# Local attention layers: the probabilities are turned in 32x32 blocks by VectorE and by DMAs through DRAM, with a new step order on every engine

## The chip, the core and the metric

The kernel runs on one core of one Trainium2 chip. The metric is the device time of one execution in microseconds (us). TensorE is PE, VectorE DVE, ScalarE ACT, GpSimd POOL, and SyncE (SP) issues the DMAs.

## The reference, cut to what matters

```python
x = x + 0.5 * ffn(layernorm(x))          # "ffn": two local layers
x = x + attn(layernorm(x), weight)       # global attention, 16 heads of 16
x = x + 0.5 * ffn(layernorm(x))
# one local layer, x of 8 x 512 x 256, 8 heads of 64, blocks of 128 tokens:
q, k, v = split(shift_token(x) @ wqkv)
q, k = rotary_xpos(l2norm(q) * qs, l2norm(k) * ksc)
sim  = q * 8 @ k.T      # a block of queries sees its own block of keys and the one before
attn = softmax(where(mask, -max, sim))
x    = x + (attn @ v) @ wo
h    = layernorm(shift_token(x)) * lg + lb
a, g = split(h @ w1 + b1);  x = x + (a * gelu(g)) @ w2 + b2
```

Everything is float32. Matrix products of weights are made of three products of rounded halves (`three`: hi by hi, lo by hi, hi by lo), the products inside attention of one float32 product.

## The kernel before

The kernel has three stages: a call of the two local layers, the global attention, and the local layers again. A local call is 16 rounds; a round is one sequence of 512 tokens through one layer, so rounds 0 to 7 are layer 1 and 8 to 15 layer 2. Rounds 3 to 6 and 9 to 14 are loops, the others are written out.

Within a round every engine works through a table of steps (`PE_STEPS`, `ACT_STEPS`, `DVE_STEPS`, `POOL_STEPS`). A name is a kind of step and a number; `+` marks a step of the next round, `-` one of the round before. So the attention of round n, the projections of round n+1 and the feed-forward part of round n-1 lie in one another. An engine keeps to its table strictly, and semaphores tie the tables together. The steps that matter here:

- z: PE turns x (bank for `zh`, `zl`, which split it into halves on ACT and DVE). q, k, v: projections, six products of 512 columns each. Q, K: PE turns the rotated q and k; `Qc`, `Kc` copy them out on ACT.
- sq, sk, ss: squares (ACT) and their sums (DVE). p: `rinv`, a power, on POOL. rq, rk: rotary on DVE. b, d: the sum of its two parts on POOL. c: k times `rinv`, on DVE (L1089).
- Attention goes by eight units i, each two heads by two query blocks; an even unit has 3, an odd one 4 blocks of 128x128 per head. S: scores on PE (L1514). X: mask and row maximum on DVE (L1106). E: exp on ACT (L848). R: reciprocal on DVE. N: scaling of the probabilities on POOL (L703). T: PE turns the 6 or 8 blocks into two PSUM banks (L1524). H, L: ACT (L855) and DVE (L1125) copy one bank each into `pT`. A: attn @ v on PE (L1544). O, P: its halves; W: times wo.
- n: PE turns the normalised rows; nh, nl: halves; x, l, r, j: residual and layer norm on DVE, s: its power on POOL. g, a: the w1 products; G: gelu on ACT; y: DVE; u, ul: halves on ACT and POOL; w: the w2 product; F, e: end of the round on DVE.
- B: PE multiplies ln_b by w1 for the bias (L1461), in rounds with `load`, that is rounds 0 and 8 of each call; i and f are casts of new weights into halves (ACT, then DVE), i0, i1 those of wqkv in round 7 (`switch`), i2 wo's, f0 to f2 those of w1 and w2.

PSUM has eight banks: RB0, RB1 for projections and scores, TB0, TB1 for what is turned, AV and UB for attention and feed-forward, and two (ACC) for W and w. `bank_before` finds in PE's table the step that last used a bank, and PE waits until that step's readers are done. ACT has to load a table (ACT_TABLE_LOAD) when it goes from exp to gelu or back.

In the global stage `y_turn` (L1257) already turns 32x32 blocks on DVE, stores them to DRAM and loads them back by rows. SP works through one queue of DMAs in the order of the code, and waits in that order too.

Of the kernel before, what the change touches and what calls it, by code (L numbers as in the profile page):

```python
# [13 lines left out]
P = 128  # L14
# [12 lines left out]
LAYERS = 2  # L27
ROUNDS = LAYERS * B
# [12 lines left out]
ACT_STEPS = ("vh1 -G0 -u0 -G1 Qc3 Kc2 vh2 -G2 -u1 Kc3 E0 E1 -G3 H0 -u2 vh3 -G4 E2 i0 -u3 H1 E3 i2 E4 i1 H2 O0 "
             "H3 E5 O1 H4 E6 -u4 E7 +zh0 +zh1 H5 -G5 +sq0 -u5 H6 +sk0 +sk1 +sq1 H7 O2 O3 f0 f1 f2 +sk2 +sq2 "
             "+Kc0 +Qc0 +vh0 +Qc1 +Qc2 +sk3 +Kc1 +sq3 nh0 nh1").split()

DVE_STEPS = ("ss3 rq3 -y0 c2 Y -y1 c3 X0 -y2 X1 R0 X2 i0 -y3 R1 X3 L0 R2 -y4 L1 X4 i2 R3 L2 X5 i1 P0 R4 L3 X6 "
             "R5 L4 X7 R6 P1 R7 L5 +zl0 +zl1 -y5 L6 +rq0 +rk0 +ss0 -F -e +rk1 +ss1 L7 +c0 P2 +rq1 P3 +c1 x B f0 "
             "l +rk2 +rq2 r f1 +ss2 j0 j1 +rk3 nl0 nl1 f2").split()


POOL_STEPS = ("b3 d3 -ul0 -ul1 N0 -ul2 N1 N2 N3 N4 -ul3 N5 -ul4 N6 -ul5 +b0 +d0 N7 +p0 +d1 +p1 +b1 +d2 +b2 s +p2 "
              "+p3").split()
# [13 lines left out]
             34: "+c0", 36: "+c1", 37: "+rq2", 39: "+rk2", 40: "+ss2", 45: "+rq3", 47: "+rk3", 48: "+ss3",  # L73
             49: "+c2", 53: "+c3", 54: "+Y"}
AHEAD_POOL = {28: "+b0", 29: "+d0", 30: "+b1", 31: "+pq0", 32: "+pk0", 33: "+d1", 34: "+pq1", 35: "+pk1", 38: "+b2",
              40: "+d2", 41: "+pq2", 42: "+pk2", 46: "+b3", 48: "+d3", 49: "+pq3", 50: "+pk3"}
BEGUN_PE, BEGUN_ACT = {64: "S0", 66: "S1"}, {66: "E0", 68: "E1"}
BEGUN_DVE, BEGUN_POOL = {65: "X0", 67: "X1", 69: "R0", 71: "X2 R1"}, {69: "N0", 72: "N1"}
# [64 lines left out]
def build(nc, ctx, x, g_w, wqkv, q_scale, k_scale, wo, ln_g, ln_b, w1, b1, w2, b2, tables, out):  # L143
# [86 lines left out]
    with ExitStack() as first:  # L230
# [25 lines left out]
    pT = sb("pT", [P, 2, 2, 4 * P], c=ffn_mem)  # L256
# [5 lines left out]
    hid = [sb(f"hid_{s}", [P, 2, N], F32R, ffn_mem) for s in ("hi", "lo")]  # L262
    ffn_mem.close()
# [18 lines left out]
    SQ = 32  # L282
# [17 lines left out]
    AV = psum[:, 4, :]  # L300
    UB = psum[:, 5, :]
    PAIR = [AV, UB]
# [32 lines left out]
    def rounds(eng, call, start, a_round, first, last):  # L335
# [6 lines left out]
        a_round(n0 + 1)  # L342
# [80 lines left out]
    def _(sp):  # L423
# [10 lines left out]
        def w_qkv(stage):  # L434
# [33 lines left out]
        def w_2(stage):  # L468
# [3 lines left out]
            sp.wait_ge(S["bias_mm"], stage + 1)  # L472
# [51 lines left out]
        KEPT, ROWS = 16 * 3 * 2 * NT, 16 * 8  # L524
# [27 lines left out]
        for call in range(2):  # L552
# [3 lines left out]
            def a_round(n, prev=True, nxt=True, load=None, switch=None, final=0, layer=0, call=call):  # L556
# [4 lines left out]
                if prev and final:  # L561
                    x_old(n - 1, call)
                if switch is not None:
                    w_qkv(switch)
                if load is not None:
                    if load % LAYERS:
                        w_o(load)
                    w_1(load, 0)
                if nxt:
                    x_ahead(n + 1, 16 * (n + 2 - B) if final or switch is not None or load is not None and load % LAYERS else None)  # L570
                if load is not None:
                    w_vectors(load)
                    w_1(load, 1)
                if prev:
                    keep(n - 1, final, call)
                x_residual(n)
                if load is not None:
                    w_2(load)
                shift(n)
# [1109 lines left out]
```

## Time and profile before

| | |
|---|---|
| median of 3 runs (lowest to highest) | 3877.69 us (3873.23 to 3880.48) |
| the profiled execution | 3879.25 us, span 3877.7 us |
| mean granted TensorE clock, share of full speed | 0.977 |
| busy share: PE, DVE, ACT, POOL | 95%, 68%, 55%, 55% |
| DMA | 160.83 MB, mean 41 GB/s |

The span is the time from the first to the last instruction; the rest of an execution's time lies around it. A share of busy time is a mean over stages: the first local call lasts from the start to about 1330 us, the global stage to about 2540 us, the second local call to the end.

### The profile page before, as it was taken

How to read it: one execution, taken by the hardware profiler on the slowest of the kernel's cores; microseconds unless marked ns; L12 is line 12 of the kernel's file. 1: busy time of each engine (PE TensorE's matmuls, PEld its weight loads, DVE VectorE, ACT ScalarE, POOL GpSimd, SP SyncE). 2: the span in 40 equal slices, each digit the busy share in tenths (PEclk: the TensorE clock that was granted, in tenths of full speed). 3: DMA queues.
4: the chain of work that ended last, by engine and by line, in shares of the span. 5: the costliest groups of instructions: out<-in, count | busy, mean ns of one | idle time of the engine just before them, and what ended most of it. 6: DMA issues, size and time to landing. Idle time of an engine off the chain costs nothing.

```text
span 3877.7 us, 74739 instructions
## 1 busy us (share of the span) xinstructions
PE 3673.6 (95%) x23040; PEld 3021.9 (78%) x23040; DVE 2620.7 (68%) x7110; ACT 2128.3 (55%) x5040; POOL 2146.7 (55%) x2179
## 2 busy tenths in 40 slices
PE   3899999999999799999999999998999999899997
PEld 2688777877787678888888888876887878777876
DVE  6678777777778555565555655666787777777774
ACT  2575676556766444444444444445756765567564
POOL 3456555555666355555555555654565555556663
PEclk8899999999999999999999999998999999999998
DMA  4001001111011222212212212101010011110110
GB/s 145 16 20 34 24 19 42 51 35 35 24 35 43 52 65 67 44 44 51 55 44 45 64 47 55 56 20 45 20 36 22 19 42 51 35 35 24 35 32 25
DMA packets 245009, 160.83 MB, mean 41 GB/s; under 512 B 122748, under 2 KB 225800, under 8 KB 244744
## 3 DMA queue, kind: packets, MB, share of 16 engines
q1 hardware_dynamic: 244744, 157.62, 14.7%
q8 instruction: 127, 2.08, 0.2%
q14 instruction: 138, 1.13, 0.1%
HBM read 107.24 MB, written 41.94 MB: 38 GB/s over the span
## 4 chain that ended last, share of the span: by engine, by line
PE 83%; DVE 6%; issue 5%; POOL 3%; ACT 2%; DMA 1%; SPq 0%; POOLq 0%; DVEq 0%; ACTq 0%
PE psum L1400 21%; PE psum L1401 19%; PE psum L1402 19%; PE psum L1514 6%; PE psum L1524 5%; PE psum L1544 5%; PE psum L1503 3%; PE psum L1630 3%; POOL ge_lo L742 1%; DVE turned_sin L1072 1%; DVE turned_qk L1068 1%; PE psum L1480 1%; DVE ssq L1079 1%; ACT squares L829 1%; PE psum L1461 1%
## 5 line engine op out<-in xcount | busy, mean ns | idle before, releaser
L742 POOL TENSOR_TENSOR ge_lo<-ge,ge_hi 128x512 fp32r<-128x512 f32 x512 | 672.7, 1316 | 531.3 <-PE psum L1402 287.7
L703 POOL TENSOR_SCALAR probs<-probs,rz 128x256 f32<-128x256 f32 (+1 forms) x1024 | 455.8, 464 | 401.7 <-DVE rz L1120 401.7
L926 ACT ACTIVATE ge<-psum 128x512 f32<-128x512 f32 x512 | 306.5, 599 | 670.2 <-PE psum L1630 667.9
L1292 DVE CAST ge_hi<-ge 128x512 fp32r<-128x512 f32 x512 | 264.1, 519 | 500.4 <-ACT ge L926 498.0
L848 ACT ACTIVATE probs<-probs,nb,rq 128x256 f32<-128x256 f32 (+1 forms) x1024 | 575.9, 565 | 30.9 <-DVE nb L1114 30.0
L1106 DVE CUSTOM_DVE_ANT_0 probs<-psum,mask 128x256 f32<-128x256 f32 (+1 forms) x1024 | 339.9, 388 | 263.9 <-PE psum L1514 263.4
L685 POOL TENSOR_TENSOR rinv<-ssq,minus_half 128x16 f32<-128x16 f32 x124 | 375.1, 3025 | 124.1 <-DVE ssq L1083 123.8
L1400 PE MATMUL psum<-wqkv_hi,hT_hi 128*128 128x512 f32 x768 | 328.4, 428 | 14.7 <-DVE hT_lo L1057 6.2
L715 POOL TENSOR_TENSOR hid_lo<-gate,hid_hi 128x512 fp32r<-128x512 f32 x160 | 206.2, 1289 | 213.6 <-ACT hid_hi L880 213.6
L829 ACT ACTIVATE squares<-psum 128x512 f32<-128x512 f32 x256 | 153.7, 602 | 302.6 <-PE psum L1402 294.1
L1401 PE MATMUL psum<-wqkv_hi,hT_lo 128*128 128x512 f32 x768 | 309.2, 403 | 0.0
L1402 PE MATMUL psum<-wqkv_lo,hT_hi 128*128 128x512 f32 x768 | 308.5, 402 | 0.0
L1400 PE MATMUL psum<-nT_hi,w_hi 128*128 128x512 f32 x704 | 292.7, 416 | 15.2 <-DVE gate L1180 13.5
L1400 PE MATMUL psum<-gw,w_hi 128*128 128x256 f32 x1024 | 287.6, 281 | 0.7 <-DVE gx L1311 0.7
L1401 PE MATMUL psum<-gw,w_lo 128*128 128x256 f32 x1024 | 287.8, 281 | 0.0
L1402 PE MATMUL psum<-gw,w_hi 128*128 128x256 f32 x1024 | 287.6, 281 | 0.0
L1402 PE MATMUL psum<-nT_lo,w_hi 128*128 128x512 f32 x704 | 280.8, 399 | 0.0
L1401 PE MATMUL psum<-nT_hi,w_lo 128*128 128x512 f32 x704 | 280.7, 399 | 0.0
L680 POOL TENSOR_TENSOR turned_qk<-turned_qk,turned_sin 128x512 f32<-128x512 f32 x128 | 166.0, 1297 | 198.8 <-DVE turned_sin L1072 198.8
L1514 PE MATMUL psum<-kT,qT 64*128 64x256 f32 (+1 forms) x2048 | 267.0, 379 | 8.3 <-DVE mx L1106 4.1
L1524 PE MATMUL psum<-ident,probs 128*128 128x128 f32 x1792 | 244.4, 277 | 15.2 <-DVE pT L1125 6.2
L1400 PE MATMUL psum<-w_hi,hid_hi 128*128 128x256 f32 x768 | 231.9, 302 | 9.1 <-POOL hid_lo L715 9.1
(156 smaller groups left out, 10288.4 us busy)
## 6 DMA issues: line engine op xcount, KB each, us to landing
xnext<-stream SPq DMA_DIRECT2D x32, 512.0 KB, 4.4
xmid<-stream SPq DMA_DIRECT2D x32, 512.0 KB, 3.8
gaT<-y_turned SPq DMA_DIRECT2D x256, 64.0 KB, 2.0
y_turned<-probs SPq DMA_DIRECT2D x192, 64.0 KB, 2.9
stream<-xmid SPq DMA_DIRECT2D x16, 512.0 KB, 2.9
wo_hi<-y_turned SPq DMA_DIRECT2D x128, 64.0 KB, 2.0
wo_lo<-y_turned SPq DMA_DIRECT2D x128, 64.0 KB, 2.0
nrm<-xmid SPq DMA_DIRECT2D x32, 224.0 KB
```

The costliest lines, as they stand in the source:

```text
L685: nc.gpsimd.tensor_tensor(rinv[:, i, :], ssq[:, i, :], minus_half[:], ALU.pow).then_inc(S["pool_r"], 1)
L703: last = nc.gpsimd.tensor_scalar(pu, pu, rz[:, h, t:t + 1], 1.0, ALU.mult, ALU.mult)
L742: nc.gpsimd.tensor_tensor(ges[1][:, k % 4, :], ge[:, k % 4, :], f32(ges[0][:, k % 4, :]), ALU.subtract).then_inc(S["g_lo"], 1)
L848: last = nc.scalar.activation(pu, pu, ACT.Exp, bias=nb[:, h, t:t + 1], scale=rq[:, 0, t, h:h + 1], accum_out=zs[:, h, t:t + 1])
L926: nc.scalar.activation(ge[:, k % 4, :], RB[k % 2], ACT.Exp, scale=GSCALE, accum_out=gz[:, h, t:t + 1]).then_inc(S["g_exp"], 1)
L1106: last = V.tensor_tensor_reduce(probs[:, i % 3, 2 * side + b, a:], RB[side][:, b * 2 * P + a:(b + 1) * 2 * P], mask[:, a:], 1.0, -3e38, AL ...
L1292: V.tensor_copy(ges[0][:, k % 4, :], ge[:, k % 4, :]).then_inc(S["g_hi"], 1)
L1400: mm(out_, lhs[0], rhs[0], start=start, stop=False, **kw)
L1401: mm(out_, lhs[1], rhs[0], start=False, stop=False, **kw)
L1402: return mm(out_, lhs[0], rhs[1], start=False, stop=stop, **kw)
L1514: last = mm(RB[side][:, b * 2 * P + a:(b + 1) * 2 * P], qT[rows, i // 2, t * P:(t + 1) * P], kT[rows, i // 2, (t - 1) * P + a:(t + 1) * P] ...
L1524: last = turn(TB[side][:, col * P:(col + 1) * P], probs[:, i % 3, 2 * side + t - blocks[0], a:a + P], ident[:])
```

## The change

Six things change in the local layers; the global stage keeps its code, but for the places where the second call's first round is begun in it.

1. T, H and L are gone. Step V (DVE) turns the 32x32 blocks of a unit's probabilities in place of their order, into `p_blocks`. SP stores the unit to DRAM (`st`, one DMA of 384 or 512 KB) and loads it back as `pT` (`ld`, four DMAs, one for each 32 partitions). A reads `pT` through a pattern (block, quarter, 32 columns) in place of contiguous columns.
2. c moves from DVE to POOL.
3. A table `BANKS` gives every PE step its PSUM bank; six banks are shared by all steps.
4. All tables have a new order, and SP has one (`SP_STEPS`).
5. B is done in the first call only (`load in range(LAYERS)`); the bias of the second call is that of the first, kept. Its vectors aren't loaded again either.
6. The rows of wqkv for layer 2 are loaded in round 1 (`early`) in place of round 7, and the casts i and f stand at other places of the tables.

```diff
+PE_STEPS = ("Q2 v1 v2 S0 K2 Q3 K3 v3 +z0 +z1 S1 -n0 -n1 +k0 +q0 S2 -g0 -a0 -g1 +q1 -a1 S3 S4 -w0 -g2 -g3 S5 S6 "
...
+DVE_STEPS = ("X0 -j0 +zl0 -j1 +zl1 X1 R0 -nl0 -nl1 i0 i1 +rk0 X2 R1 V0 +rq0 -y0 +ss0 V1 -y1 X3 R2 X4 i2 +rq1 V2 "
...
+SP_STEPS = ("+xin wq wo wf0 st0 st1 ld0 ld1 -old st2 st3 ld2 st4 ld3 st5 st6 ld4 wf1 ld5 st7 ld6 ld7 -keep res "
+            "shift wf2").split()
...
+BANKS = {"z": (2, 4),
+         "k": (4, 5, 1, 2),
+         "S": (2, 0, 0, 2, 4, 4, 0, 0),
...
+        def p_keep(m, i):
+            w, turn_ = unit_blocks(i) * P, UNITS // 2 * m + i // 2
+            need_apart(sp, (S["dve_v"], UNITS * m + i + 1), (S[f"p_in{i % 2}"], 16 * P // SQ * (turn_ - 1)))
+            sp.dma_start(p_turned[i % 4, :, 0:w], p_blocks[:, unit_columns(i)]).then_inc(S[f"p_kept{i % 2}"], 16)
+        def p_rows(m, i):
+            w, turn_ = unit_blocks(i) * P, UNITS // 2 * m + i // 2
+            need_apart(sp, (S[f"p_kept{i % 2}"], 16 * (turn_ + 1)), (S["pe_av"], UNITS * m + i - 1))
+            q = P // SQ
+            for k in range(q):
+                sp.dma_start(pT[k * SQ:(k + 1) * SQ, unit_columns(i)].rearrange("c (q x) -> c q x", q=q),
+                             p_turned[i % 4, :, k * w // q:(k + 1) * w // q].rearrange("(q c) x -> c q x", q=q)
+                             ).then_inc(S[f"p_in{i % 2}"], 16)
...
+                if kind == "c":
+                    nc.gpsimd.tensor_tensor(kv, kv, rinv[:, i, HEADS:2 * HEADS].unsqueeze(2).to_broadcast([P, HEADS, DH]),
+                                            ALU.mult).then_inc(S["pool_c"], 1)
...
-                if kind == "L":
-                    V.tensor_copy(pT[:, i % 2, 1, 0:w], TB[1][:, 0:w]).then_inc(S["dve_p"], 1)
+                if kind == "V":
+                        last = V.transpose(turned[:, js], kept[:, first * P:(first + js.stop - js.start) * P].rearrange(
+                            "p (j k c) -> p j k c", k=P // SQ, c=SQ))
...
-                if kind == "T":
-                            last = turn(TB[side][:, col * P:(col + 1) * P],
-                                        probs[:, i % 3, 2 * side + t - blocks[0], a:a + P], ident[:])
...
-                    pe.wait_ge(S["act_p"], UNITS * m + i + 1)
-                    pe.wait_ge(S["dve_p"], UNITS * m + i + 1)
+                    pe.wait_ge(S[f"p_in{i % 2}"], 16 * P // SQ * (UNITS // 2 * m + i // 2 + 1))
+                    rows = pT[:, unit_columns(i)].rearrange("p (q j r) -> p j q r", q=P // SQ, r=SQ)
...
-                if kind == "B" and load is not None:
+                if kind == "B" and load in range(LAYERS):
```

On PE, in the loop over the rounds of the first layer, this stands before around A2, A3 and T4 (`pT,vs` is A, `ident,probs` T, `kT,qT` S):

```order
L154 REGISTER_ALU
L1537 ISA
L1544 MATMUL psum<-pT,vs 64x256 x2
L1544 MATMUL psum<-pT,vs 64x128 x4
L1544 MATMUL psum<-pT,vs 64x256 x2
L1544 MATMUL psum<-pT,vs 64x128 x2
L1524 MATMUL psum<-ident,probs 128x128 x6
L154 ISA
L154 REGISTER_ALU
L1514 MATMUL psum<-kT,qT 128x256 x4
```

and this in the changed kernel around A0, A1 (`nT` with `w` is a g or a step, `w` with `hid` a w step):

```order
L1446 MATMUL psum<-nT_hi,w_hi 128x512
L1447 MATMUL psum<-nT_hi,w_lo 128x512
L1448 MATMUL psum<-nT_lo,w_hi 128x512
L176 ISA
L1574 REGISTER_ALU
L1582 MATMUL psum<-pT,vs 64x256 x2
L1582 MATMUL psum<-pT,vs 64x128 x4
L1582 MATMUL psum<-pT,vs 64x256 x2
L1582 MATMUL psum<-pT,vs 64x128 x2
L1446 MATMUL psum<-w_hi,hid_hi 128x256
L1447 MATMUL psum<-w_hi,hid_lo 128x256
```

Between A and the next S there stood a T; now A follows on feed-forward steps and is followed by one, and no T is left.

On ACT, in the same loop, the stretch around the gelus G3 and G4 was (L848 is exp, L874 gelu, L855 the copy H, L880 u, L833 a copy of v):

```order
L868 REGISTER_ALU
L874 ACT_TABLE_LOAD
L874 ACTIVATE gate<-psum,b1t 128x512
L853 ISA
L154 REGISTER_ALU
L855 COPY pT<-psum 128x384
L880 CAST hid_hi<-gate 128x512
L833 COPY vs<-psum 128x512
L868 REGISTER_ALU
L874 ACTIVATE gate<-psum,b1t 128x512
L842 REGISTER_ALU
L848 ACT_TABLE_LOAD
```

and the stretch around G0 and G1 is now (L910 is exp, L931 gelu, L937 u):

```order
L925 REGISTER_ALU
L176 REGISTER_ALU
L931 ACT_TABLE_LOAD
L931 ACTIVATE gate<-psum,b1t 128x512
L925 REGISTER_ALU
L931 ACTIVATE gate<-psum,b1t 128x512
L937 CAST hid_hi<-gate 128x512
L904 REGISTER_ALU
L910 ACT_TABLE_LOAD
L910 ACTIVATE probs,zs<-probs,nb,rq 128x128
L910 ACTIVATE probs,zs<-probs,nb,rq 128x256
L910 ACTIVATE probs,zs<-probs,nb,rq 128x128
```

The gelus lie at other places among the exps: a loop round had four table loads and has six. The copies H are gone.

On SP the loop round of before held six DMAs, which these rows show:

```order
L494 DMA xnext<-stream 128x4x256
L154 ISA
L522 ISA
L522 DMA stream<-xmid 128x4x256
L154 ISA
L499 ISA
L499 DMA xmid<-stream 128x4x256
L154 ISA
L154 REGISTER_ALU
L506 DMA nrm<-xmid 112x4x128
L507 DMA nrm<-xmid 15x4x128
L508 DMA nrm<-xmid 1x3x128
```

The changed round begins so (`p_turned<-p_blocks` is st, `pT<-p_turned` ld):

```order
L176 ISA x2
L562 DMA p_turned<-p_blocks 128x768
L176 REGISTER_ALU
L562 DMA p_turned<-p_blocks 128x1024
L176 ISA
L176 REGISTER_ALU
L570 DMA pT<-p_turned 32x4x192 x4
L570 DMA pT<-p_turned 32x4x256 x4
L176 REGISTER_ALU x2
L562 DMA p_turned<-p_blocks 128x768
```

Forty DMAs more stand in a round, all ahead of the store of the round before (`keep`) and the load of `xmid`, in one queue with them.

## Rows read from the trace of the kernel before

**Rows 1.** Page, part 1: busy us, share of the span, instructions

```profile
PE 3673.6 (95%) x23040; PEld 3021.9 (78%) x23040; DVE 2620.7 (68%) x7110; ACT 2128.3 (55%) x5040; POOL 2146.7 (55%) x2179
```

**Rows 2.** Windows: stretch, length, busy us of PE, PEld, DVE, ACT, POOL, clock, DMA

```profile
210.20:583.40 373.20, 372.15 (x2532) 301.05 (x2531) 284.02 (x821) 247.32 (x581) 223.04 (x256) 1.00 0.08 25
837.80:1215.90 378.10, 373.56 (x2533) 300.69 (x2531) 290.02 (x831) 247.46 (x581) 228.06 (x256) 1.00 0.10 31
...
583.40:666.80 83.40, 76.97 (x508) 61.74 (x507) 60.58 (x173) 52.51 (x119) 44.60 (x52) 0.96 0.14 49
742.80:837.80 95.00, 85.39 (x556) 69.49 (x555) 62.89 (x174) 53.69 (x123) 45.75 (x52) 0.89 0.11 33
...
44.00:113.50 69.50, 49.78 (x259) 35.72 (x259) 37.94 (x116) 31.36 (x85) 32.53 (x36) 0.83 0.11 30
```

**Rows 3.** Waits of PE, 803 to 1200 us: total us, times, longest

```profile
PE psum L1400 <- DVE xmid L1200: 3.5, 5, 0.9
```

**Rows 4.** Timeline of PE in one round: start us, us

```profile
568.80 1.03 PE L1524 MATMUL psum<-ident,probs 128*128 128x128 f32 x8
569.76 0.93 PE L1514 MATMUL psum<-kT,qT 64*128 64x128 f32 x8
...
572.29 0.88 PE L1524 MATMUL psum<-ident,probs 128*128 128x128 f32 x6
573.09 1.14 PE L1514 MATMUL psum<-kT,qT 64*128 64x256 f32 x8
...
588.61 0.39 PE L1400 MATMUL psum<-wqkv_hi,hT_hi 128*128 128x512 f32 x1
588.84 0.40 PE L1401 MATMUL psum<-wqkv_hi,hT_lo 128*128 128x512 f32 x1
```

**Rows 5.** Groups by line, five rounds, 210.2 to 583.4 us

```profile
L1544 PE MATMUL psum<-pT,vs 128*64 128x128 f32 (+1 forms) x400 | 35.9, 322 | 0.0
L1089 DVE TENSOR_TENSOR turned_qk<-turned_qk,rinv 128x512 f32<-128x512 f32 x20 | 27.6, 1379 | 3.5 <-POOL rinv L685 2.4 <-POOL turned_qk L680 1.1
L1125 DVE COPY pT<-psum 128x512 f32<-128x512 f32 (+1 forms) x40 | 24.7, 618 | 5.2 <-PE psum L1524 5.2
L848 ACT ACT_TABLE_LOAD x10 | 12.8, 1283 | 0.2
```

**Rows 6.** Source line 1257 (y_turn): duration ns min/median/max

```profile
L1257 DVE STREAM_TRANSPOSE probs<-gy_hi x4: 1236/1240/1245, 1309.0 to 2197.3; 128x1024 f32<-128x1024 f32 x4
```

**Rows 7.** Timelines of DVE and POOL, 472 to 478 us

```profile
472.83 0.68 DVE L1089 TENSOR_TENSOR turned_qk<-turned_qk,rinv 128x512 f32<-128x512 f32 x1
476.01 1.77 DVE L1089 TENSOR_TENSOR turned_qk<-turned_qk,rinv 128x512 f32<-128x512 f32 x1 [0.29 <-POOL turned_qk L680]
...
475.94 1.28 POOL L715 TENSOR_TENSOR hid_lo<-gate,hid_hi 128x512 fp32r<-128x512 f32 x1
```

**Rows 8.** Timeline of DVE, other steps of such a round

```profile
465.10 1.11 DVE L1163 TENSOR_SCALAR nrm<-nrm,mv,rs 128x128 f32<-128x128 f32 x4
...
511.63 1.28 DVE L1057 TENSOR_TENSOR hT_lo<-psum,hT_hi 128x512 fp32r<-128x512 f32 x2
```

**Rows 9.** Timeline of ACT: start of one exp unit and of the next

```profile
495.39 0.60 ACT L848 ACTIVATE probs<-probs,nb,rq 128x256 f32<-128x256 f32 x1
...
497.75 0.49 ACT L848 ACTIVATE probs<-probs,nb,rq 128x128 f32<-128x128 f32 x1
```

**Rows 10.** Page, part 6: KB each, us from issue to landing

```profile
xnext<-stream SPq DMA_DIRECT2D x32, 512.0 KB, 4.4
...
stream<-xmid SPq DMA_DIRECT2D x16, 512.0 KB, 2.9
```

**Rows 11.** Timeline of PE, a round with new weights (768 us)

```profile
768.14 6.33 PE L1461 MATMUL psum<-lnp,wbuf 128*128 128x1 f32 x48
...
785.43 1.97 PE L1503 MATMUL psum<-ident,turned_qk 128*128 128x128 f32 x8 [7.40 <-ACT qT L838]
```

**Rows 12.** Groups by line, whole span: a cast of the weights

```profile
L977 DVE TENSOR_TENSOR wqkv_lo<-wbuf,wqkv_hi 128x1536 fp32r<-128x1536 f32 x8 | 14.7, 1854 | 17.0 <-ACT wqkv_hi L766 17.0
```

More of the change, by code:

```diff
@@ L34 @@
 SHIFTED = P - 16
[L41 to L49, printed above, removed]
@@ L554, in first, with a_round @@
                 x_ahead(n, None)
-            def a_round(n, prev=True, nxt=True, load=None, switch=None, final=0, layer=0, call=call):
+            def a_round(n, prev=True, nxt=True, load=None, switch=None, final=0, layer=0, call=call, early=None):
                 if call == 0 and not nxt:
@@ L560, in a_round @@
                         sp.dma_start(gx[b][:], tokens(x_mid[0], b)).then_inc(S["g_in"], 16)
[L561 to L566, printed above, removed]
-                        w_o(load)
[L568 to L579, printed above, removed]
+                fresh = final or switch is not None or load is not None and load % LAYERS
+                if early is not None:
+                    w_qkv_rows(early)
+                for kind, i, m in steps(SP_STEPS, n, prev, nxt):
+                    if kind == "old" and final:
+                        x_old(m, call)
+                    if kind == "wq" and switch is not None:
+                        w_qkv(switch)
+                    if kind == "wo" and load is not None and load % LAYERS:
+                        w_o(load)
+                    if kind == "wf" and load is not None:
+                        if i == 1 and load < LAYERS:
+                            w_vectors(load)
+                        if i < KD:
+                            w_1(load, i)
+                        else:
+                            w_2(load)
+                    if kind == "xin":
+                        x_ahead(m, 16 * (m + 1 - B) if fresh else None)
+                    if kind == "keep":
+                        keep(m, final, call)
+                    if kind == "res":
+                        x_residual(m)
+                    if kind == "st":
+                        p_keep(m, i)
+                    if kind == "ld":
+                        p_rows(m, i)
+                    if kind == "shift":
+                        shift(m)
             def last(m, final, call=call):
@@ L724, in first, with a_round @@
                 some_steps(n - 1, False, True, 1)
-            def a_round(n, prev=True, nxt=True, load=None, switch=None, final=0, layer=0, call=call):
+            def a_round(n, prev=True, nxt=True, load=None, switch=None, final=0, layer=0, call=call, early=None):
                 some_steps(n, prev, nxt, table=prepared(left(POOL_STEPS, BEGUN_POOL, load), PREP_POOL, call, nxt))
@@ L901, in first, with a_round @@
                 some_steps(n - 1, False, True, 1)
-            def a_round(n, prev=True, nxt=True, load=None, switch=None, final=0, layer=0, call=call):
+            def a_round(n, prev=True, nxt=True, load=None, switch=None, final=0, layer=0, call=call, early=None):
                 some_steps(n, prev, nxt, None, load, switch, layer,
@@ L1263, in first, with a_round @@
                 some_steps(n - 1, False, True, 1)
-            def a_round(n, prev=True, nxt=True, load=None, switch=None, final=0, layer=0, call=call):
+            def a_round(n, prev=True, nxt=True, load=None, switch=None, final=0, layer=0, call=call, early=None):
                 some_steps(n, prev, nxt, None, load, switch, final, layer,
@@ L1385, in bank_before @@
             behind = ahead + turns - line[at][2]
-            if first_n == ROUNDS and n is not None and n + behind == ROUNDS and k in "zqkvQK":
+            if k == "B" or first_n == ROUNDS and n is not None and n + behind == ROUNDS and k in "zqkvQK":
                 continue
@@ L1486, in some_steps @@
                         fresh_qkv = None
-                    if w == 2 and i == 0 and load is not None and not ahead:
-                        pe.wait_ge(S["bias_ok"], load + 1)
                     for kt in range(KD):
@@ L1513, in some_steps @@
                             rows = slice(side * DH, (side + 1) * DH)
-                            last = mm(RB[side][:, b * 2 * P + a:(b + 1) * 2 * P], qT[rows, i // 2, t * P:(t + 1) * P],
+                            last = mm(bank("S", i, side)[:, b * 2 * P + a:(b + 1) * 2 * P], qT[rows, i // 2, t * P:(t + 1) * P],
                                       kT[rows, i // 2, (t - 1) * P + a:(t + 1) * P], start=True, stop=True)
@@ L1573, in some_steps @@
                         lo = (i if c else FJ + i) * P
-                        last = three((UB, AV)[c], [w_[:, kt, lo:lo + P] for w_ in w1_s], [h[:, kt, :] for h in nT],
+                        last = three(bank(kind, i), [w_[:, kt, lo:lo + P] for w_ in w1_s], [h[:, kt, :] for h in nT],
                                      kt == 0, kt == KD - 1)
@@ L1587, in some_steps @@
                     last.then_inc(S["pe_w2"], 1)
-                if kind == "B" and load is not None:
+                if kind == "B" and load in range(LAYERS):
                     biases(load)
+                    biased = False
             return fresh_w1, fresh_w2
@@ L1598, in first, with a_round @@
                 some_steps(n - 1, False, True, call, 1)
-            def a_round(n, prev=True, nxt=True, load=None, switch=None, final=0, layer=0, call=call):
+            def a_round(n, prev=True, nxt=True, load=None, switch=None, final=0, layer=0, call=call, early=None):
                 some_steps(n, prev, nxt, call, None, load, switch, left(PE_STEPS, BEGUN_PE, load))
```

228 lines of the change are left out of this document (122 added, 106 removed).

## The prediction

> **What bounds the kernel now.** I read the busy shares first: PE 95% of the span, DVE 68%, ACT and POOL 55% [rows 1]. A mean hides stages, so next the windows. Five rounds of the first layer last 373.2 us, 74.6 each, with PE busy for 372.15 of them at full clock; five of the second last 378.1, 75.6 each, with PE busy for 373.56 [rows 2]. The list of PE's waits says where second-layer rounds lose time: 0.9 us at most before a W or w step, on the final add of DVE (L1200) [rows 3]. So in 24 of 32 rounds PE is the bound and nothing but its own work counts. In the rest it isn't: the round with the switch of weights lasts 83.4, the one with `load` 95.0 with the clock at 0.89, and the first only has PE busy for 49.8 of 69.5 us at 0.83 [rows 2]. The second call I take to repeat the first.
>
> **What leaves PE.** From the start of an eight-block T to the next step 0.96 us pass, 0.80 with six blocks [rows 4]. A round has four of each: 7.04 us. This is real path in the 24 rounds: 74.6 - 7.0 = 67.6.
>
> **What A costs now.** It has as many matmuls of as many columns; only the reading pattern is broken into runs of 32. No row shows such a read. Bounds: 0 extra, or A's 7.2 us twice [rows 5]. I take 0, since the runs are still contiguous 128 bytes; the double is a rival.
>
> **The other engines have room.** Per round of the first layer DVE is busy 284.02/5 = 56.8 us [rows 2]. L goes (24.7/5 = 4.9) and c goes (27.6/5 = 5.5) [rows 5]. V comes: 1.24 us for 1024 elements in y_turn [rows 6], estimated 0.95 for the 768 of an even unit, so 4 x 2.2 = 8.8. That gives 55.2 of 67.6. POOL: 223.04/5 = 44.6 [rows 2], plus four c at 1.3, the price of its 512-element op with two inputs [rows 7]: 49.8. ACT: 247.32/5 = 49.5 [rows 2], less the copies H, which I price like L's, 4.9, plus two more table loads at 1.28 [rows 5]: 47.2. SP issues 40 DMAs more. None becomes the bound by sum.
>
> **Whether each is in time.** I laid one round of the new tables beside PE's. PE's steps: six products at 0.23 apart make 1.4 us [rows 4]. Time 0 is the end of S0. The first tight place is the start: PE would reach k0 at 5.6, but k0 has bank 4, which was z1's, so it waits for zl1. DVE does X0, j0 (1.1), zl0 (0.64), j1, zl1 [rows 8]. zl0 waits for ACT: PE ends v3 at 2.8, and vh3 and zh0 behind it take half a us each, so zh0 is done at about 3.9; X0 and j0 are done by then. So zl0 ends at 4.6, j1 at 5.6, zl1 at 6.3. **New stall: 0.7 us a round.**
>
> Then ACT's chain, an odd exp unit taking 2.36 us [rows 9], an even one estimated at 2.14, a load 1.28: E0 ends at 7.9, E1 11.7, G1 15.0, E2 19.3, E3 22.6, G2 24.5, E4 28.6, E5 31.4. Against that PE wants G1's bank at 15.6 (a1), G2's at 25.3 (a2), and S7 needs X6, done at 30.1, at 31.7. Slacks: 0.6, 0.8, 1.6 us. They hold, but closely.
>
> **The probabilities' trip.** st takes 2.9 us as the store of 512 KB does, ld 4.4 as the load of 512 KB does [rows 10], plus some 0.2 for each handoff: 7.7 from V to A. V7 ends at about 45.5, A7 is due at 57.7: 4.5 us spare. The loads are tied also to A of the unit two before, since `pT` has two halves: A5 ends at 49.1, so ld7 lands at 53.7, 4.0 spare; A2 to A4 have 7.8 for 4.6. Hidden, at 0. If the cover goes, each late us costs PE one.
>
> SP stands still where ld7 waits for A5, and `keep`, the reload of xmid and the shift stand behind it. e is done at 53.4, later than that, so nothing waits for SP there; keep 2.9 and reload 4.4 make 60.9, x needs xmid at 63.
>
> A steady round is thus 67.6 + 0.7 = 68.3. The layer-2 wait on the last add should go, since F now ends four us before e: also 68.3. **24 rounds: 12 x 6.3 + 12 x 7.3 = 163 us.**
>
> **Rounds with weights.** Switch: both casts of wqkv now stand right before k0. ACT reaches them at 8.8; DVE does the rotary tables, then two casts at 1.85 [rows 12], done at about 14.7 against 6.3: 8.4 us, and perhaps 4 of half clock after such a gap: 68.3 + 12.4 = 80.7 against 83.4. Gain 5 in two rounds.
>
> Load, first call: B (6.33 us) stays, the wait that follows it was 7.40 [rows 11], and w2's load still follows B and the shift. I take the excess over a plain round, 95.0 - 75.6 = 19.4, as unchanged: gain 7. Second call: no B, but f2 waits for w2's load, issued after f0 and the shift at 67.6 and landed at 71.5; v2 stands behind it in PE, 6.6 us late, plus 2.5 of half clock: 77.4 against 95. Gain 18. Together 25.
>
> First rounds: PE has slack there, and the trip adds about 7.5 us after E7, covered by projections. I take 3 for the first call; in the second B and half of its after-effects add 11: 17. Last rounds have no projections to cover the trip: T's 7 us less an exposed 5: 2 each, 4.
>
> **Sum:** 163 + 5 + 25 + 17 + 4 = 214 us. The profiled execution took 3879.25 us (1.6 above the median): 3665.
>
> **A rule against it.** An eight-block T holds PE for 0.96 us and V holds DVE for 1.24 with a trip of 7.7 behind it [rows 4, 6, 10]. The Trainium skill's page "VectorE: DVE Perf Modes" (Rules for kernel authors) says to use TensorE for a 128x128 transpose when PSUM will do, and calls DVE's 32x32 form right only within blocks. By latency alone the rule is right here and the change loses 8 us a unit; by the bound engine it isn't. The rival "trip exposed" is what it would look like.
>
> **Rivals.**
> 1. *The port.* c alone takes 0.68 us on DVE, and 1.77 when POOL's `hid_lo` began 0.07 before it; it ends 0.5 after POOL's op [rows 7]. If V is held like that, each of V0, V1 and V3, ahead of X3 and X5, waits 0.65 on average for POOL's ops of 1.3: 2 us a round, of which 0.5 is slack. 24 x 1.5 = 36: 3701. Against it: V has one input, and y_turn's four times lie within 9 ns of each other [rows 6]. The Trainium skill's "SBUF — State Buffer" (SBUF: two separate sides) says that a GpSimd op locks out a DVE op with two SBUF inputs or in a two-port mode; by that rule c pays, as the rows show, and V doesn't. Chance 0.18.
> 2. *The softmax chain leads.* If my spacings are short by 10% over the 28.6 us to E4, S7 comes 1.3 us late after its slack and the gelus' banks 2 more: some 3 us a round, 24 x 3 = 72: 3737. Six table loads and slacks under 1 us speak for it; each duration taken from start-to-start rows against. Chance 0.13.
> 3. *A is slower through its pattern.* A is 35.9/5 = 7.2 us a round [rows 5]. Doubled, it eats what the T's gave: 3665 + 32 x 7.2 = 3895, and half of that doubling leaves half of the gain. Chance 0.05.
> 4. *The trip exposed (the other side).* One mechanism: ld (i+2) can't start before A(i) ends, and three such legs (A0 to A2, A2 to A4, A4 to A6) of 7.8 to 8.2 us stand in a row each round. A leg of L us costs 3 x (L - 8). Against a gain of 6.7 a round it decides from L = 10.2, where I have 4.6. With four DMAs of 128 pieces each at 1 KB queued behind a store, L of 11 would give 3 x 3 x 32 = 288 less 214: 3953. Chance 0.05.
>
> **Numbers.** Forecast (3625 to 3690) 0.57, rivals 0.18, 0.13, 0.05, 0.05; 0.02 that the changed transitions or the clock spoil more. Low end: T's busy share is 7.5 and no stall, 24 x 1.2 = 29 less, and some for transitions: 3625. High end: rival 2 with its rounding: 3755. A change of under 0.2% (8 us) can't be told from none. Faster: forecast, rivals 1 and 2 and part of 3: 0.91. Same 0.04, slower 0.05.
>
> **What would show it.** Right: no matmul on probs; the windows of five rounds near 342 us with PE over 98% busy; STREAM_TRANSPOSE near 1.2 us on odd units; PE's waits headed by `hT_lo` (zl) with 0.7 each; matmuls on pT with an unchanged mean; c on POOL near 1.3. Wrong: PE waiting on `pT` from DMA (rival 4), on `gate` or `mx` for 1 to 3 us each round (rival 2), V at 1.8 and more (rival 1), longer matmuls on pT (rival 3), half clock inside plain rounds.

## The result, and the profile after

The changed kernel takes 3776.25 us (median of 4 runs, 3775.53 to 3784.34) against 3878.72 for the kernel before (4 runs, 3873.23 to 3880.48): ratio 0.9743, 95% interval 0.9726 to 0.976. It is 102 us faster; 214 us less were forecast (3665, with a range of 3625 to 3755). The profiled executions are 95.1 us apart in span, 3877.7 and 3782.6, and the account below is made with these.

The profile of the changed kernel, part 1 (as in [rows 1]) and part 4, the chain that ended last:

```profile
PE 3475.8 (92%) x21152; PEld 2843.0 (75%) x21152; DVE 2639.0 (70%) x7104; ACT 2076.9 (55%) x4840; POOL 2267.5 (60%) x2307
...
PE 61%; DVE 14%; issue 10%; ACT 7%; POOL 4%; DMA 2%; SPq 1%; DVEq 1%; ACTq 0%; POOLq 0%
```

PE is busy for 198 us less (32 rounds of T at 7.04 us are 225), but half of that came back as waiting. The chain tells the kind: before the change "issue", time in which an engine waits for nothing that the profile shows, was 5% of it, now 10%.

Windows of the changed kernel (columns as in [rows 2]), each from the S0 of one round to the S0 of the next. In order: rounds 3, 6 and 12 of the first call, round 12 of the second (rounds are counted from 1 from here on, not from 0 as ahead of the prediction: 1 to 8 of a call are layer 1, 9 to 16 layer 2), the switch round of the first call, the two rounds with `load` for layer 2, the first round of the second call, and the last one:

```profile
232.24:301.31 69.07, 67.78 (x451) 54.53 (x450) 55.43 (x167) 48.09 (x110) 48.31 (x56) 1.00 0.42 134
444.33:517.29 72.96, 68.31 (x451) 54.50 (x451) 55.37 (x166) 48.25 (x110) 48.26 (x56) 1.00 0.40 126
907.32:977.15 69.83, 68.09 (x451) 54.46 (x450) 61.16 (x167) 48.11 (x110) 49.11 (x56) 1.00 0.43 139
3372.41:3447.54 75.13, 69.78 (x451) 55.59 (x450) 61.25 (x168) 48.27 (x110) 49.12 (x56) 0.98 0.41 130
590.37:669.44 79.07, 69.37 (x451) 55.67 (x450) 60.83 (x174) 50.94 (x112) 48.39 (x56) 0.94 0.39 125
669.44:767.82 98.38, 82.93 (x499) 67.10 (x498) 64.21 (x181) 53.72 (x117) 51.68 (x57) 0.84 0.41 126
3136.47:3227.88 91.41, 74.04 (x451) 58.99 (x450) 63.67 (x178) 53.71 (x117) 51.70 (x57) 0.89 0.43 136
2538.83:2640.87 102.04, 59.60 (x341) 46.02 (x340) 61.52 (x179) 35.94 (x93) 43.94 (x50) 0.77 0.43 137
3672.72:3782.60 109.88, 81.54 (x503) 64.22 (x502) 51.77 (x168) 47.93 (x107) 33.05 (x47) 0.91 0.29 94
```

Compare the first row with the second, and the third with the fourth: the same instructions on every engine (a record or two is missing), and 3.9 and 5.3 us more. It is not chance. The plain first-layer rounds of the second call are all like the first row, and the plain second-layer ones of the first call all like the third; slow are just the rounds after a jump back of the loop in the first call's layer 1 (three) and in the second call's layer 2 (five).

From the starts of S0 in both traces, the gain of the spans, summed by kind of round:

| rounds | forecast gain | measured |
|---|---|---|
| 8 plain rounds that turned out slow (3 + 5) | 55.4 | 7.1 |
| 16 other plain rounds | 107.8 | 90.2 |
| 2 with the switch | 5 | 7.7 |
| 2 with `load` for layer 2 | 25 | 3.0 |
| first and last rounds, with all between and before | 21 | -12.9 |
| sum | 214 | 95.1 |

Where the eight rounds lose it, the timelines of VectorE and then of TensorE show (start, us), in round 11 of the second call:

```profile
3299.31 0.17 DVE L1208 TENSOR_SCALAR ve<-mv 128x4 f32<-128x4 f32 x1
3302.93 0.29 DVE L1152 CUSTOM_DVE_ANT_0 probs<-psum,mask 128x128 f32<-128x128 f32 x1 [3.45 <-issue]
...
3304.91 0.42 DVE L1152 CUSTOM_DVE_ANT_0 probs<-psum,mask 128x256 f32<-128x256 f32 x1 [1.12 <-issue]
```

```profile
3303.71 1.09 PE L1533 MATMUL psum<-ident,xnext 128*128 128x128 f32 x8 [2.63 <-DVE mx L1152]
...
3310.04 0.63 PE L1446 MATMUL psum<-wqkv_hi,hT_hi 128*128 128x512 f32 x1
3310.47 0.63 PE L1447 MATMUL psum<-wqkv_hi,hT_lo 128*128 128x512 f32 x1
```

L1208 is the last thing in VectorE's table, X0 (L1152) the first: between them lies the jump back of the loop. VectorE does nothing for 3.45 us there, and 1.12 more inside X0. TensorE's z0 has the bank of S0, whose scores X0 reads, so it waits 2.63; six us later the products are at 0.43 us from start to start instead of 0.23 for some 3 us, the lower of the two clocks. In the same place of a fast round the idle time ahead of X0 is 0.7 us.

What VectorE waits for has no row among the waits. The DMA queues have it (packets, MB, share of 16 engines), first for 3299 to 3374 us, a slow round, then for 909 to 979, a fast one, where q1 is all there is:

```profile
q1 hardware_dynamic: 8373, 9.66, 39.9%
q14 instruction: 5, 0.04, 0.1%
```

```profile
q1 hardware_dynamic: 8419, 9.70, 43.4%
```

Five packets of 8 KB of instructions are fetched in the slow round and none in the fast one. The whole traces hold 187 such packets now and 138 before, those of all engines that this queue serves.

### The profile page after: what moved, and what is told of

It reads as the page before. It is cut to its first block, busy times and chain, and to the rows that moved or that the text cites. A ratio compares the mean times of both kernels' runs of the same rounds, so it can differ in the third digit from the quotient of the medians.

```text
span 3782.6 us, 72921 instructions
## 1 busy us (share of the span) xinstructions
PE 3475.8 (92%) x21152; PEld 2843.0 (75%) x21152; DVE 2639.0 (70%) x7104; ACT 2076.9 (55%) x4840; POOL 2267.5 (60%) x2307
## 3 DMA queue, kind: packets, MB, share of 16 engines
q14 instruction: 187, 1.53, 0.1%
## 4 chain that ended last, share of the span: by engine, by line
PE 61%; DVE 14%; issue 10%; ACT 7%; POOL 4%; DMA 2%; SPq 1%; DVEq 1%; ACTq 0%; POOLq 0%
PE psum L1446 17%; PE psum L1447 16%; PE psum L1448 16%; PE psum L1582 4%; DVE probs L1152 3%; PE psum L1668 3%; ACT probs L910 3%; PE psum L1554 2%; DVE p_blocks L1174 1%; PE psum L1565 1%; POOL probs L770 1%; ACT L910 1%; DVE turned_qk L1121 1%; DVE nb L1160 1%; POOL ge_lo L809 1%
## 5 line engine op out<-in xcount | busy, mean ns | idle before, releaser
L770 POOL TENSOR_SCALAR probs<-probs,rz 128x256 f32<-128x256 f32 (+1 forms) x1024 | 444.0, 453 | 557.6 <-DVE rz L1166 557.6
L1343 DVE CAST ge_hi<-ge 128x512 fp32r<-128x512 f32 x512 | 266.0, 522 | 505.8 <-ACT ge L983 503.8
L910 ACT ACTIVATE probs<-probs,nb,rq 128x256 f32<-128x256 f32 (+1 forms) x1024 | 574.8, 564 | 51.0 <-DVE nb L1160 49.8
L1152 DVE CUSTOM_DVE_ANT_0 probs<-psum,mask 128x256 f32<-128x256 f32 (+1 forms) x1024 | 336.7, 383 | 96.0 <-issue 47.0
L745 POOL TENSOR_TENSOR rinv<-ssq,minus_half 128x16 f32<-128x16 f32 x124 | 366.2, 2954 | 24.4 <-DVE ssq L1136 17.5
L1446 PE MATMUL psum<-wqkv_hi,hT_hi 128*128 128x512 f32 x768 | 341.7, 445 | 27.0 <-issue 16.8
L1174 DVE STREAM_TRANSPOSE p_blocks<-probs 128x384 f32<-128x384 f32 (+1 forms) x384 | 291.2, 784 | 62.3 <-POOL probs L770 59.6
L1565 PE MATMUL psum<-kT,qT 64*128 64x256 f32 (+1 forms) x2048 | 253.1, 377 | 19.8 <-DVE mx L1152 11.7
L1582 PE MATMUL psum<-pT,vs 128*64 128x128 f32 (+1 forms) x2560 | 231.3, 327 | 29.6 <-DMA pT<-p_turned 25.0
L1121 DVE TENSOR_TENSOR turned_qk<-psum,rope 128x512 f32<-128x512 f32 x256 | 173.2, 677 | 92.3 <-ACT squares L891 72.4
```

The source lines that it names most:

```text
L745: nc.gpsimd.tensor_tensor(rinv[:, i, :], ssq[:, i, :], minus_half[:], ALU.pow).then_inc(S["pool_r"], 1)
L770: last = nc.gpsimd.tensor_scalar(pu, pu, rz[:, h, t:t + 1], 1.0, ALU.mult, ALU.mult)
L910: last = nc.scalar.activation(pu, pu, ACT.Exp, bias=nb[:, h, t:t + 1], scale=rq[:, 0, t, h:h + 1], accum_out=zs[:, h, t:t + 1])
L1152: last = V.tensor_tensor_reduce(probs[:, i % 3, 2 * side + b, a:], bank("S", i, side)[:, b * 2 * P + a:(b + 1) * 2 * P], mask[:, a:], 1.0, ...
L1174: last = V.transpose(turned[:, js], kept[:, first * P:(first + js.stop - js.start) * P].rearrange("p (j k c) -> p j k c", k=P // SQ, c=SQ))
L1446: mm(out_, lhs[0], rhs[0], start=start, stop=False, **kw)
```

## Experiments

**Where the loops' code lies.** In straight-line code the trace shows an 8 KB fetch about a microsecond after every 128th instruction of VectorE (from 15 us to the first loop nine times out of nine, each within 1.6 us). Call such a stretch of 128 instructions a page of code. Counted in these pages, VectorE's four round loops of the changed kernel (275 to 277 instructions each) begin at places 113, 92, 13 and 116 of a page. 113 + 275 and 116 + 277 exceed 384, so these two touch four pages, the others three. Theory A: a loop that touches four pages is fetched again at each jump back. Theory B: the softmax chain or the probabilities' trip is what leads in the slow rounds. The test is to shift the program and nothing else:

```
         V = nc.vector
+        for _ in range(50):                       # 25, 105
+            dve.sem_inc(S["apart"], 1)
```

> The changed kernel with 50 semaphore increments ahead of VectorE's program, nothing else, so that everything VectorE runs lies 50 instructions further on. Theory A (the loop's code): counted in pages of 128 instructions from the points where the trace fetches 8 KB, VectorE's body of 275 to 277 instructions begins at places 113, 92, 13 and 116 of a page in the four round loops; the first and the last touch four pages and are fetched anew at each jump back (3 to 4 us without an instruction), the other two touch three and are not. 50 further on all four touch three: no pause is left, rounds 5 to 7 of layer 1 in the first call fall from 73.2 to 69.4 us and rounds 11 to 15 of layer 2 in the second call from 75.1 to 69.8, 12 and 27 us less: 3776 - 38 = 3738 (3732 to 3745), and the 8 KB instruction packets fall from 187 to about 145. Theory B (the softmax chain or the probabilities' trip leads in those rounds): the padding changes nothing, 3776.

> As before with 25 increments. Theory A: only the layer-2 loop of the first call begins late enough in a page (117) to touch four, so its rounds 11 to 15 rise from 69.8 to about 75 us while the eight slow rounds of the changed kernel fall to 69.4 and 69.8: 3776 - 38 + 26 = 3764. Theory B: no round changes, 3776.

> As before with 105 increments. Theory A: only the layer-1 loop of the second call touches four pages (place 118), so three of its rounds rise from 69.4 to about 73 us and all others are at 69.4 and 69.8: 3776 - 38 + 11 = 3749. Theory B: no round changes, 3776.

Measured: 50 increments 3741.58 us (5 runs, 3740.62 to 3746.5; ratio to before 0.9652, 0.9639 to 0.9666), 25 increments 3761.15 and 105 increments 3763.41 (one run each). Windows of one round: with 50 round 6 of the first call and round 12 of the second, with 25 round 11 of the first, with 105 round 5 of the second:

```profile
443.06:512.47 69.41, 68.01 (x451) 54.57 (x450) 55.24 (x166) 48.08 (x110) 48.37 (x56) 1.00 0.40 132
3356.38:3426.11 69.73, 68.09 (x451) 54.45 (x450) 61.23 (x168) 48.09 (x110) 49.25 (x56) 1.00 0.43 139
```

```profile
824.05:898.06 74.01, 69.50 (x451) 55.17 (x451) 61.20 (x168) 48.28 (x110) 49.12 (x56) 0.98 0.41 132
```

```profile
2840.95:2914.52 73.57, 69.60 (x452) 55.21 (x451) 55.39 (x166) 48.27 (x110) 48.37 (x56) 0.98 0.38 125
```

With 50 all eight slow rounds are fast, and the 8 KB packets are 146 in all (170 with 25, 161 with 105). With 25 only the second-layer loop of the first call is slow (five rounds at 74.0 to 75.1), with 105 only the first-layer loop of the second call (three at 73.6 to 75.3), as expected of four pages at places 117 and 118. Theory A stands, B falls. With 105 the time is 14 us above what I expected: 4.6 because the three jumps cost 4.2 to 5.9 instead of 3.7, 4.3 because the first S0 comes later (VectorE's first operation starts at 11.0 us, behind twice the increments, instead of 5.5), and 3.6 because the padded kernel is itself above its 3738.

The kernel before, moved in the same way:

> The kernel before, with 50 increments ahead of VectorE's program. Theory A: its loops begin at places 110, 72, 101 and 63 with 267 to 269 instructions, all in three pages; 50 further on the layer-2 loop of the first call (122) touches four, so VectorE pauses 3 to 4 us at five jumps back. There PE has c2's transpose due only 1.3 us after c2, so 1 to 3 us of each pause should reach PE: rounds 11 to 15 of the first call at 76.7 to 78.7 instead of 75.7, 3879 + 5 to 15. Theory B: nothing changes, 3879. If the time doesn't change although the pause is there, the place of the loop's end in the table decides whether it costs.

It takes 3907.17 us (4 runs, 3902.4 to 3910.46; ratio 1.0083, 1.0068 to 1.0098). Round 12 of the first call with the increments, then VectorE at one jump, its wait and TensorE's waits over the loop:

```profile
966.16:1048.11 81.95, 77.28 (x507) 62.07 (x507) 57.69 (x166) 49.51 (x116) 45.59 (x51) 0.96 0.09 29
...
875.18 1.28 DVE L1081 TENSOR_REDUCE ssq<-squares 128x8 f32<-128x512 f32 x2 [4.53 <-issue]
...
DVE ssq L1081 <- issue: 23.4, 5, 4.8
PE psum L1402 <- DVE gate L1182: 18.6, 5, 3.8
```

The same round without them:

```profile
957.69:1033.47 75.78, 74.73 (x507) 60.17 (x507) 58.08 (x167) 49.52 (x117) 45.55 (x51) 1.00 0.10 31
```

So the loop that I expected at place 122 does pause, five times 4.7 us, and no other does. What that costs I had mis-sized, 1 to 3 us a jump where 6 were measured, so the time lies 13 us above the 3884 to 3894 that I expected. TensorE doesn't wait at K2, as I thought, but 3.7 us for the gate (L1182) behind it, and the clock granted over the round is 0.96. Fifty instructions that do nothing make the tuned kernel 0.8% slower. All 24 round loops of the six kernels up to here obey the count: the five in four pages pause (two of the changed kernel, one in each of three padded ones), the nineteen in three pages don't.

**The first round of the second call.** Its waits in the changed kernel (engine, line, releaser: us, times, longest):

```profile
PE psum L1533 <- DMA xnext<-stream: 13.7, 1, 13.7
PE psum L1554 <- DVE w_lo L1034: 10.9, 1, 10.9
PE psum L1582 <- DMA pT<-p_turned: 5.8, 3, 2.6
PE psum L1565 <- DVE mx L1152: 5.3, 2, 3.9
```

SyncE issues xnext's load behind the global layer's last two stores. Before the change z0 stood at the end of the round and this was early enough; now z0 stands at its start. The edit, on the padded kernel (the load at its old place, behind the stores, is left out in this round):

```
                 sequences(sp, sequence)
+                need_apart(sp, (S["g_out"], 16 * 2 + 1), (S["pe_z"], KD * (ROUNDS + 1)))
+                sp.dma_start(xnext[:], tokens(stream, ROUNDS + 1)).then_inc(S["x_in"], 16)
                 store(B - 1, 1)
```

> The padded version (50 increments), and in the second call's first round the load of xnext for round 2 is issued ahead of the global layer's last two stores instead of behind them. In the changed kernel TensorE waits there 13.7 us for this load before z0, since SyncE issues it only behind the last store. Theory A: the round loses this wait, minus what comes late next (scores' maxima, probabilities' loads): 8 to 13.7 us less, 3741.6 - 11 = 3731. Theory B (the round is bound by VectorE's and SyncE's own chains, so the wait only moves): under 3 us less, 3740.

3733.02 us (4 runs, 3731.07 to 3736.38; ratio 0.9625, 0.9608 to 0.9641). The round goes from 102.84 us in the padded kernel to 91.19, 11.6 less. The wait of 13.7 is gone, and the one for `hT_lo` right behind it has grown from 1.5 to 7.2. Theory A, within its range. Over the whole kernel the medians are 8.6 us apart.

**The rounds with `load`.** TensorE waits at their end for the last cast of w2, behind a load that is issued behind the shift. The edit, for the two load rounds of the second call:

```
-ACT  ... O2 +sq3 O3 f0 f1          DVE  ... +rk2 +rq3 P2 P3 +ss3 x B f0 +rk3 +Y f1 l r f2    SP  ... res shift wf2
+ACT  ... f0 O2 +sq3 O3 f1          DVE  ... +rk2 f0 +rq3 P2 P3 +ss3 x B +rk3 +Y f1 f2 l r    SP  ... res wf2 shift
```

> The padded version, and in the two load rounds of the second call the cast f0 stands ahead of x (behind rk2), w2's load ahead of the shift, and f2 ahead of l. In the changed kernel TensorE waits 10.9 and 11.2 us at the end of these rounds for f2, whose load is issued behind the shift. Theory A: w2 lands some 5 us earlier, so each of the two waits falls to about 6: 10 us less, 3732. Theory B: the next round can't begin earlier anyway, because the norm (l, r, s) behind x ends at the same time: under 3 us less, 3740.

3730.66 us (4 runs, 3729.84 to 3733.8; ratio 0.9618, 0.9602 to 0.9634). The two rounds lose 5.3 and 5.4 us (102.84 to 97.58, 90.81 to 85.43), and the wait of 11.2 is 7.0. Theory A.

**The probabilities' trip.** Extra stores of the same size ahead of each st. The unit's loads wait for all of them, and so does the next V that writes the same half of `p_blocks`:

```
+            for spare in range(1):                # 2
+                sp.dma_start(p_spare[4 * spare + i % 4, :, 0:w], p_blocks[:, unit_columns(i)]
+                             ).then_inc(S[f"p_kept{i % 2}"], 16)
             sp.dma_start(p_turned[i % 4, :, 0:w], ...
```

> The padded version with one more store of the same size ahead of each st, to a spare tensor (the loads of a unit wait for both): the probabilities' trip gets about 2.9 us longer. Theory A (the trip is hidden with 4 us to spare, as predicted): plain rounds stay at 69.4 and 69.7 us, the load and last rounds get 1 to 3 us longer each: 3742 + 5 to 20. Theory B (the trip is already at its limit): plain rounds grow by 2.9 or more, 3742 + 70 and up.

> As before with two more stores, 5.8 us longer. Theory A: the 4 us are used up, TensorE waits for pT in every plain round, 1 to 6 us of it: 3742 + 24 to 150, and the waits stand on the first matmuls on pT. Theory B (more than 6 us to spare): plain rounds unchanged, 3742 + 10 to 30.

3768.65 us with one, 3943.39 with two (one run each). A plain round of the second layer with one and A3 in it, then with two and what TensorE and VectorE wait for in it:

```profile
905.70:975.40 69.70, 68.11 (x451) 54.47 (x450) 60.52 (x165) 48.10 (x110) 48.85 (x56) 1.00 0.57 192
...
947.25 1.09 PE L1587 MATMUL psum<-pT,vs 128*64 128x128 f32 x12 [0.28 <-DMA pT<-p_turned]
```

```profile
963.61:1040.07 76.46, 70.24 (x451) 55.68 (x450) 59.41 (x173) 48.16 (x110) 49.78 (x56) 0.98 0.63 223
...
PE psum L1587 <- DMA pT<-p_turned: 4.7, 2, 4.0
...
DVE p_blocks L1179 <- DMA p_turned<-p_blocks: 4.5, 2, 2.7
```

With one the plain rounds take 69.3 to 70.3 us (once 71.5), 0.4 more on average than in the padded kernel, with two 73.7 to 77.7. How much the stores added the row of the store says: its 512 KB land 2.6 us after the issue, then 4.2, then 5.4, so less than in proportion, and each one's issue takes some 0.4. That makes 2.0 and 3.6 us. With 2.0 more, A3 or A5 waits 0.1 to 1.0 us for pT in 16 of the 24 plain rounds, where the padded kernel has no such wait. So these two had some 1.0 to 1.9 us spare, an estimate from the two numbers. The prediction had looked for the tight place at A7 (4.0 spare) and at the legs of the even units (7.8 for 4.6). Of the 22 us between this span and the padded one's 11 lie in the 24 plain rounds, the rest in the first, switch and last ones.

That is theory A in kind, but both times lie above its ranges (3747 to 3762, and 3766 to 3892). The run with two stores doesn't measure the trip alone either: VectorE waits 4.5 us before V in the round shown, until the stores of an earlier unit have read `p_blocks`, 124 us in the whole kernel; with one store it is 6.5 us in the whole kernel. How its 143 us in the plain rounds divide between that wait and the longer trip no run shows.

**All of it, and one more wait.** The padding, the early xnext and the early f0 together, and on top of that A0 ahead of a2:

> The padding, the early xnext load and the early f0 together. If the three act in different places their gains add: 35 us of the padding, 10.5 and 13 of the other two by their ratios to the kernel before (0.9652, 0.9625, 0.9618): ratio 0.959, about 3720 us. If the first round of the second call has one bound under both of the last two, less than the sum there: 3722 to 3726.

> As the one before, and in TensorE's table A0 stands ahead of a2 and a3 instead of behind them. In nearly every round TensorE waits 0.8 us at a2 for ScalarE's gelu G2, whose PSUM bank a2 takes; A0 (0.9 us) would cover that. Theory A (that wait is all of it): 0.8 us less in 30 rounds, 24 us less than the one before, 3697. Theory B (the softmax chain sets the pace behind it, so what a2 gains S7 or A0's own load gives back): under 6 us less, 3715 or more, with the wait now on scores' maxima or on pT.

Together: 3724.05 us (5 runs, 3720.58 to 3725.54; ratio 0.9606, 0.9593 to 0.9619), 52 us under the changed kernel. That is 4 us above the full sum; the second call's first round takes 86.89 us, where the two edits would leave 85.9 if they added. With A0 first: 3731.5 us (4 runs, 3728.66 to 3738.11; ratio 0.9626, 0.9611 to 0.9641), no gain. One plain round of each, TensorE's two waits in it, first with all three edits, then with A0 first:

```profile
1043.07 0.66 PE L1613 MATMUL psum<-ident,nrm 128*128 128x128 f32 x4 [0.67 <-DVE nrm L1227]
1063.45 0.50 PE L1459 MATMUL psum<-nT_hi,w_hi 128*128 128x512 f32 x1 [0.79 <-ACT gate L942]
```

```profile
1048.08 0.66 PE L1613 MATMUL psum<-ident,nrm 128*128 128x128 f32 x4 [0.68 <-DVE nrm L1227]
1068.70 0.87 PE L1595 MATMUL psum<-pT,vs 128*64 128x256 f32 x8 [0.99 <-DVE mx L1165]
```

The wait for the gelu is gone, and A0 waits a little longer for the scores' maxima of S5, whose bank it takes. Theory B: the bank that the gelu G2 frees and the one that X5 frees come within 0.3 us of each other there.

## Why the prediction was right or wrong

**The step that failed** is "24 rounds: 12 x 6.3 + 12 x 7.3 = 163 us", from "None becomes the bound by sum" and a round laid out by hand that every repetition was to follow. A term was missing: the fetch of the engine's own code, put at nothing without a reason. VectorE's loop body grew from some 268 to 276 instructions and came to lie elsewhere; two of four loops touch a fourth page of 128 and pause at each jump back. Eight of the 24 rounds gained 7.1 us together where I had 55.4; of the 48 missing the padding gives back 38 (their lengths add up to 595.2 us in the changed kernel and 556.8 in the padded one), and the other 10 are the mis-sized plain round below. No rival named it. The new order isn't to blame: the jump now stands right ahead of X0, on which z0 depends, but the padded kernel before paid 6 us a jump in the old order too. The kernel before happened to lie well.

Of the 119 us between forecast and measured gain these pauses are the largest single part, 38, and without them the kernel takes 3741.58 us, within the range. They aren't all of it: 28 come from the plain round, 34 from the first and last rounds, 22 from the load rounds, and the switch rounds give 3 back.

**The plain round** of 68.3 was mis-sized by a little: 69.1 to 69.4 in the first layer and 69.3 to 69.8 in the second. "What leaves PE" is right: busy 67.8 and 68.1, where I had 67.6. The stall of 0.7 on `hT_lo` is not there, but n0 ahead of it waits 0.5 to 0.7 for the norm, so this term had the right size by luck. The slack of 0.8 that I gave a2 is a wait of 0.8, which is rival 2 in small: 0.8 us a round instead of 3, and the last experiment shows how close the chains lie. Together a plain round takes 1.2 us more than forecast. In the second layer another 0.2 to 0.4 for `turned_sin` stand in place of the wait on the last add. In the 16 rounds without a pause this made 18 us.

**A, V and c** by their groups over the whole span (busy, mean ns), and V's durations (ns, min/median/max):

```profile
L1582 PE MATMUL psum<-pT,vs 128*64 128x128 f32 (+1 forms) x2560 | 231.3, 327 | 29.6 <-DMA pT<-p_turned 25.0 <-DVE oT_lo L1179 4.6
...
L760 POOL TENSOR_TENSOR turned_qk<-turned_qk,rinv 128x512 f32<-128x512 f32 x128 | 138.3, 1080 | 4.9
...
L1174 DVE STREAM_TRANSPOSE p_blocks<-probs x384: 527/578/1248, 90.6 to 3715.2; 128x384 f32<-128x384 f32 x128, 128x1024 f32<-128x1024 f32 x64
```

A at no extra cost was right, 327 ns for 322 [rows 5]. c takes 1.08 on POOL instead of 1.3. V is 1.24 for 1024 elements as read, and comes twice at 0.56 for the 768 of an even unit, where I had 0.95. Rival 1, the port: V's longest is 1.248 us, so nothing holds it up; rivals 3 and 4 didn't come either, and the two extra stores show what rival 4 looks like, 4.7 us of waits on pT in a round. By the page "SBUF — State Buffer" (SBUF: two separate sides) of the Trainium skill a GpSimd op holds up a DVE op that has two SBUF inputs or runs in a two-port mode; V has one input, and the row agrees. The rule of the Trainium skill's page "VectorE: DVE Perf Modes" (Rules for kernel authors), which would have had the 128x128 transposes on TensorE, didn't decide here, where TensorE was the bound: the plain rounds without a pause gained 5.2 to 6.2 us each.

**Switch rounds**: right. The forecast was 8.4 us of wait at k0 for both casts, and TensorE's waits in that round begin with them, put down to "issue":

```profile
PE psum L1446 <- issue: 8.4, 1, 8.4
```

VectorE's two casts run from 602.77 to 606.18 us, and k0 starts at 606.29. The rounds take 79.1 and 79.7 us for 80.7. The 4 us for the lower clock were too much: TensorE is busy for 69.4 us there, 1.6 more than in round 3.

**Load rounds**: the second call's direction was right and its size wrong. TensorE's waits there:

```profile
PE psum L1554 <- DVE w_lo L1034: 11.2, 1, 11.2
PE psum L1565 <- DVE turned_sin L1125: 3.0, 1, 3.0
PE psum L1582 <- DMA pT<-p_turned: 2.7, 1, 2.7
```

"6.6 us late" is 11.2, and the other two I didn't have: 91.4 us for 77.4. In the first call the excess taken "as unchanged" failed: 8.1, 3.9 and 3.0 of the same waits beside B, 98.4 for 87.7.

**First and last rounds**: 34 us of the shortfall. By the new order some 11 us of feed-forward work lie behind a round's S0 instead of ahead of it (in the last round PE is busy for 81.5 us now; before it was 77.2, of which 7 were T), so the first rounds look better by that and the last ones worse, and the sum doesn't change. Set right for that, the first call's beginning gained 4 us (3 forecast). The second call's first round is where it fails, 14 forecast and 13 lost: "PE has slack there" overlooked that z0 now stands at the start of the round while its load is issued where it was. The last rounds with what follows lost 3 and 1 where I had 2 gained each; which part of that is the trip without cover and which the global layer's start wasn't tried apart.

What stays open: why the first call's `load` round has its waits beside B (no run changed it), and how much of a jump's 4 to 6 us is the wait and how much the lower clock behind it. The windows give a first division: of the 5.3 us that round 12 of the second call takes more than round 12 of the first, 1.7 are more busy time of TensorE for the same work, and 3.6 are idle; of the 6.2 in the padded kernel before 2.6 and 3.6. No run holds the clock apart. The accounts by kind of round compare single profiled executions, and the changed kernel's lies 8 us above its median.

## What to carry to other kernels

Before judging a reordering by its rounds, compare the same round in every loop that runs it. If equal instructions take different times, look for "issue" at the jump back and for instruction packets in the DMA queues of that stretch; count where the loop's body lies, and shift it by some instructions that do nothing. And when a step moves to the front of a round, follow its load to the queue that issues it, in the first round above all, where something else stands ahead in that queue.

## What the runs showed of the hardware

At a jump back VectorE stood idle for 0.7 us or less where the loop's body touched three pages of 128 instructions, and for 3.2 to 4.8 us where it touched four. Five packets of 8 KB were fetched in such a round. In the global layer's loop, whose body is 811 instructions, 3.5 to 3.9 us pass from the operation at the jump (L1362, before L1311) to the next one (L1343, before L1292) each time that it jumps back, and 1.6 at its end, where it doesn't; this is so before and after the change. The Trainium skill's page "Runtime: NRT & Kernel Launch" (Instruction fetch mechanics) says that a taken branch whose target isn't in the engine's two-page window stalls for a fetch of that page. The traces agree with the stall, but not with its page of 16 KB, 256 instructions, for VectorE: its fetches come after every 128 instructions, q14's 187 packets hold 1.53 MB, 8 KB each, and bodies of 267 to 277 instructions went from one round to the next without a fetch in three such pages. Here the measurement decides.
